# Local layers: token shift in front of the layer norm by two SBUF-to-SBUF copies in place of two matmuls, layer norm on whole rows

## The reference

```python
def shift_token(t):
    t1, t2 = jnp.split(t, 2, axis=-1)
    t2 = jnp.pad(t2, ((0, 0), (1, 0), (0, 0)))[:, :-1]
    return jnp.concatenate([t1, t2], axis=-1)

def _layer(x, wqkv, qs, ksc, wo, lg, lb, w1, b1, w2, b2):
    h = shift_token(x)
    qkv = h @ wqkv
    ...
    o = local_attention(q, k, v)
    x = x + o @ wo
    h = shift_token(x)
    mu = h.mean(-1, keepdims=True)
    var = h.var(-1, keepdims=True)
    h = (h - mu) / jnp.sqrt(var + 1e-05) * lg + lb
    h = h @ w1 + b1
    a, g = jnp.split(h, 2, axis=-1)
    h = a * jax.nn.gelu(g, approximate=False)
    x = x + h @ w2 + b2
    return x
```

## Time and profile before

| what | value |
|---|---|
| runs shown (us) | 3350.12, 3350.09, 3436.24 |
| median | 3350.12 us |
| profiled execution | 3355.18 us |
| its span, first to last instruction | 3353.0 us |
| TensorE busy | 3150.6 us (94%) |
| VectorE busy | 2405.7 us (72%) |
| ScalarE busy | 1821.5 us (54%) |
| GpSimd busy | 1577.1 us (47%) |
| granted TensorE clock, mean | 0.980 |
| DMA, local layers | load and store of 512 KB pieces, 16 passes |

### The profile page before, as it was taken

How to read it: one execution, slowest core, us unless ns; L and a number is a source line. 1 busy time by engine, 2 the same in 40 slices (tenths; PEclk the granted TensorE clock), 3 DMA queues, 4 the chain that set the end, 5 groups by cost and what they waited for, 6 DMA issues and landing times. The chain is left out here.

```text
span 3353.0 us, 51248 instructions
## 1 busy us (share of the span) xinstructions
PE 3150.6 (94%) x16012; PEld 1862.8 (56%) x16012; DVE 2405.7 (72%) x4374; ACT 1821.5 (54%) x4275; POOL 1577.1 (47%) x969
## 2 busy tenths in 40 slices
PE   6999999999999888999999799999999999999997
PEld 3454545454454545666666466666666666666665
DVE  8999999999999897667777555555555555555553
ACT  4768686777768545555656344444444444433442
POOL 2666666666666560000000355544555455555552
PEclk8999999999999999999999899999999999999999
DMA  4767677576767573000100000000001100000000
GB/s 148 259 215 246 220 239 240 210 267 213 258 217 241 204 234 124 25 25 25 38 31 13 20 1 19 19 19 19 19 19 38 57 19 25 25 25 25 25 13 19
DMA packets 146655, 343.30 MB, mean 102 GB/s; under 512 B 14898, under 2 KB 78470, under 8 KB 146582
## 3 DMA queue, kind: packets, MB, share of 16 engines
q1 hardware_dynamic: 138134, 334.02, 29.6%
q10 hardware_dynamic: 8448, 8.39, 0.8%
HBM read 320.87 MB, written 21.50 MB: 102 GB/s over the span
## 5 line engine op out<-in xcount | busy, mean ns | idle before, releaser
L559 POOL TENSOR_TENSOR hb<-bcB,du 128x1024 f32<-128x1024 f32 x256 | 602.1, 2352 | 390.1 <-DVE hb L699 350.9
L688 DVE TENSOR_TENSOR_SCAN ps_dA<-ps_dA,hb 128x1024 f32<-128x1024 f32 x256 | 585.8, 2288 | 43.6 <-ACT ps_dA L914 43.6
L1226 PE MATMUL ps_y<-hb,ident 128*128 128x512 f32 x1024 | 491.5, 609 | 28.9 <-DVE hb L699 28.9
L2077 POOL TENSOR_TENSOR c_pr<-c_pr,c_inv 128x512 f32<-128x512 f32 (+1 forms) x256 | 233.5, 933 | 364.6 <-DVE c_inv L2194 364.6
L1609 ACT ACTIVATE b_pr<-b_ps_s,b_negmax 128x256 f32<-128x256 f32 (+1 forms) x512 | 263.4, 527 | 166.7 <-DVE b_negmax L1522 165.3
L1226 PEld LDWEIGHTS ps_y<-hb,ident 128*128 128x128 f32 x1024 | 191.4, 194 | 252.8 <-issue 190.8
L914 ACT ACTIVATE ps_dA<-delta,a_neg 128x511 f32<-128x511 f32 x512 | 330.1, 676 | 1.1
L2313 ACT ACTIVATE c_pr<-c_ps_s,c_negmax 128x256 f32<-128x256 f32 (+1 forms) x512 | 224.8, 457 | 179.0 <-DVE c_negmax L2187 178.2
L699 DVE TENSOR_TENSOR hb<-ps_dA,bcC 128x1024 f32<-128x1024 f32 x256 | 311.9, 1218 | 5.9
L2187 DVE CUSTOM_DVE_ANT_0 c_ps_s<-c_ps_s,c_mask 128x256 f32<-128x256 f32 (+1 forms) x512 | 187.6, 417 | 120.4 <-issue 120.4
L2569 PE MATMUL c_ps_s<-c_hT,c_w 128*128 128x512 f32 x576 | 261.1, 600 | 0.9 <-ACT c_hT L2369 0.9
(11 more groups left out here) (295 smaller groups left out, 6177.1 us busy)
## 6 DMA issues: line engine op xcount, KB each, us to landing
bcB<-bc_scratch SPq DMA_DIRECT2D x256, 512.0 KB, 4.6
bcC<-bc_scratch SPq DMA_DIRECT2D x256, 512.0 KB, 4.7
c_x<-stream_scratch SPq DMA_DIRECT2D x16, 512.0 KB, 5.1
c_xr<-stream_scratch SPq DMA_DIRECT2D x16, 512.0 KB, 4.3
rows<-in_x_dram SPq DMA_DIRECT2D x8, 512.0 KB, 5.6
sum<-in_x_dram SPq DMA_DIRECT2D x8, 512.0 KB, 7.7
x_scratch<-sum SPq DMA_DIRECT2D x8, 512.0 KB, 6.7
b_xb<-x_scratch SPq DMA_DIRECT2D x8, 512.0 KB, 4.7
```

Of the source, the lines that this page charges most:

```text
L559: pool.tensor_tensor(hb[:, s % RING, :, :], bcB[:, s % ROWS, :, :], bc(du[:, c % 2, :].unsqueeze(1), [P, NG, T]), ALU.mult)\
L688: dve.tensor_tensor_scan(flat(h_all), flat(h_all), flat(tile), 0.0, ALU.mult, ALU.add)\
L1226: last = pe.matmul(ps_y[:, :], W["ident"][:, :], hb[:, r % RING, i, :], start=False, stop=(g == GROUPS - 1 and i == NG - 1))
L2077: pool.tensor_tensor(rows, rows, bc(inv[:, u, :].unsqueeze(2), [P, 2, w]), ALU.mult)\
```

## The change

The right half of the sum now goes to a tile of its own, `xa_right`, the left half straight into `h`. SyncE issues two copies from SBUF to SBUF: partitions 0 to 126 of `xa_right` to partitions 1 to 127 of `h`'s right half, and partition 127 of tiles 0 to 2 to partition 0 of tiles 1 to 3. The zeros of the first token are written once at the start. VectorE waits for both copies before any statistics, and takes statistics and normalisation on whole rows of 256, four instructions each. The two matmuls, their two matrices and the wait in front of them are gone. GpSimd's `residual` adds the two halves apart. In the diff, hunks that only rename the start-up semaphore's count on other engines are left out.

```diff
@@ -1895,12 +1895,11 @@
         den = sb("c_den", [P, UNITS, 2])
         inv = sb("c_inv", [P, UNITS, 2])
         tiny = sb("c_tiny", [P, 2, NH])
-        down = sb("c_down", [P, P])
-        corner = sb("c_corner", [P, P])
         oT = sb("c_oT", [P, IC, T])
-        xa = sb("c_xa", [P, TT, D])
+        xa_right = sb("c_xa_right", [P, TT, P])
+        h = sb("c_h", [P, TT, D])
         xa2 = sb("c_xa2", [P, TT, D])
-        stats = sb("c_stats", [P, TT, 12])
+        stats = sb("c_stats", [P, TT, 6])
         mv = sb("c_mv", [P, TT, 2])
         rstd = sb("c_rstd", [P, TT])
         veps = sb("c_veps", [P, TT])
@@ -1914,9 +1913,9 @@
         ps_o = ctx.enter_context(nc.psum_tensor("c_ps_o", [P, 2, 512], F32))
         ps_x = ps_t[:, :, :].rearrange("p a (b d) -> p (a b) d", b=2)
         ps_y = ps_o[:, :, :].rearrange("p a (b d) -> p (a b) d", b=2)
-        xsh = ps_t[:, 0, :].rearrange("p (t d) -> p t d", t=TT)
 
         s_c = ctx.enter_context(nc.semaphore("c_const"))
+        CONSTANTS = 6
         rot_ready = ctx.enter_context(nc.semaphore("c_rot_ready"))
         x_in = S("c_x_in", 16, "sp")
         xr_in = S("c_xr_in", 16, "sp")
@@ -1948,13 +1947,13 @@
         oT_ready = S("c_oT_ready", IC, "act")
         wo_done = S("c_wo_done", 1, "pe")
         xa_ready = S("c_xa", 2, "dve")
-        shifted = S("c_shifted", 1, "pe")
-        v_steps = S("c_v_steps", 2 * TT + 1, "dve")
+        shifted = S("c_shifted", 32, "sp")
+        v_steps = S("c_v_steps", TT + 1, "dve")
         mv_ready = S("c_mv", TT, "dve")
         g_steps = S("c_g_steps", 1, "pool")
         rstd_ready = S("c_rstd_ready", 1, "pool")
         xa2_ready = S("c_xa2", 1, "pool")
-        hn_ready = S("c_hn", 2 * TT, "dve")
+        hn_ready = S("c_hn", TT, "dve")
         h_turned = S("c_h_turned", DC, "pe")
         hT_ready = S("c_hT_ready", DC, "act")
         ag_proj = S("c_ag_proj", JC, "pe")
@@ -1962,7 +1961,7 @@
         hid_ready = S("c_hid", JC, "dve")
         y_done = S("c_y_done", 1, "pe")
         xo_ready = S("c_xo", 1, "dve")
-        b2_added = S("c_b2_added", 1, "pool")
+        b2_added = S("c_b2_added", 2, "pool")
         base_in = S("c_base_in", 16, "act")
         stored = S("c_stored", 16, "sp")
         block = ctx.enter_context(nc.Block())
@@ -2017,6 +2017,9 @@
                         sp.wait_ge(stored.s, stored.at(it - NB + 1, 16))
                     sp.dma_start(x_sb[:, :, :], tiles(stream[nl, nb])).then_inc(x_in.s, 16)
 
+                sp.wait_ge(xa_ready.s, xa_ready.at(it, 1))
+                sp.dma_start(h[1:P, :, P:D], xa_right[0:P - 1, :, :]).then_inc(shifted.s, 16)
+                sp.dma_start(h[0:1, 1:TT, P:D], xa_right[P - 1:P, 0:TT - 1, :]).then_inc(shifted.s, 16)
                 if l < L - 1:
                     sp.wait_ge(xo_ready.s, xo_ready.at(it, 1))
                     sp.dma_start(tiles(stream[l + 1, b]), xo[:, :, :]).then_inc(stored.s, 16)
@@ -2038,15 +2041,8 @@
             pool.memset(tiny[:, :, :], 1e-24).then_inc(s_c, 1)
 
             pool.memset(hid[:, JC - 1, :], 0.0).then_inc(s_c, 1)
-            pool.memset(down[:, :], 0.0).then_inc(s_c, 1)
-            pool.memset(corner[:, :], 0.0).then_inc(s_c, 1)
-            pool.wait_ge(s_c, 7)
-
-            pool.affine_select(out=down[:, :], in_=down[:, :], compare_op=ALU.not_equal, fill=1.0,
-                               base=1, pattern=[[-1, P]], channel_multiplier=1).then_inc(s_c, 1)
-            pool.affine_select(out=corner[:, :], in_=corner[:, :], compare_op=ALU.not_equal, fill=1.0,
-                               base=P - 1, pattern=[[1, P]], channel_multiplier=-1).then_inc(s_c, 1)
-            pool.wait_ge(s_c, 9)
+            pool.memset(h[0:1, 0, P:D], 0.0).then_inc(s_c, 1)
+            pool.wait_ge(s_c, CONSTANTS)
 
             def turn_heads(n, t):
 
@@ -2081,14 +2077,16 @@
                 pool.wait_ge(s_t, 16 * 15)
                 pool.wait_ge(xa_ready.s, xa_ready.at(it, 2))
                 pool.wait_ge(xo_ready.s, xo_ready.at(it, 0))
-                ins = pool.tensor_tensor(xa2[:, :, :], xa[:, :, :], bc(b2_row[:, l, :].unsqueeze(1), [P, TT, D]), ALU.add)
+                pool.tensor_tensor(xa2[:, :, P:D], xa_right[:, :, :], bc(b2_row[:, l, P:D].unsqueeze(1), [P, TT, P]), ALU.add)\
+                    .then_inc(b2_added.s, 1)
+                ins = pool.tensor_tensor(xa2[:, :, 0:P], h[:, :, 0:P], bc(b2_row[:, l, 0:P].unsqueeze(1), [P, TT, P]), ALU.add)
+                ins.then_inc(b2_added.s, 1)
+                pool.wait_ge(b2_added.s, b2_added.at(it, 2))
                 if l == L - 1:
-
-                    ins.then_inc(b2_added.s, 1)
-                    pool.wait_ge(b2_added.s, b2_added.at(it - (L - 1) * NB, 1))
                     pool.wait_ge(base_in.s, base_in.at(it - (L - 1) * NB, 16))
-                    ins = pool.tensor_tensor(xa2[:, :, :], xa2[:, :, :], xo[:, :, :], ALU.add)
-                ins.then_inc(xa2_ready.s, 1)
+                    pool.tensor_tensor(xa2[:, :, :], xa2[:, :, :], xo[:, :, :], ALU.add).then_inc(xa2_ready.s, 1)
+                else:
+                    pool.sem_inc(xa2_ready.s, 1)
 
             def root(it):
 
@@ -2231,25 +2229,22 @@
                 dve.wait_ge(xr_in.s, xr_in.at(it, 16))
                 dve.wait_ge(xa2_ready.s, xa2_ready.at(it, 0))
                 dve.wait_ge(hn_ready.s, hn_ready.at(it, 0))
-                for half in (slice(P, D), slice(0, P)):
-                    dve.tensor_tensor(xa[:, :, half], ps_x[:, :, half], xr[:, :, half], ALU.add).then_inc(xa_ready.s, 1)
+                dve.tensor_tensor(xa_right[:, :, :], ps_x[:, :, P:D], xr[:, :, P:D], ALU.add).then_inc(xa_ready.s, 1)
+                dve.tensor_tensor(h[:, :, 0:P], ps_x[:, :, 0:P], xr[:, :, 0:P], ALU.add).then_inc(xa_ready.s, 1)
 
                 st.turn(it)
                 dve.wait_ge(xa_ready.s, xa_ready.at(it, 2))
+                dve.wait_ge(shifted.s, shifted.at(it, 32))
                 for t in range(TT):
-                    st.done(dve.bn_stats(stats[:, t, 0:6], xa[:, t, 0:P]))
-                dve.wait_ge(shifted.s, shifted.at(it, 1))
-                for t in range(TT):
-                    st.done(dve.bn_stats(stats[:, t, 6:12], xsh[:, t, :]))
-                dve.wait_ge(st.s, st.at(2 * TT))
+                    st.done(dve.bn_stats(stats[:, t, :], h[:, t, :]))
+                dve.wait_ge(st.s, st.at(TT))
                 st.done(dve.memset(tick[:, :], 0.0))
                 for t in range(TT):
                     dve.bn_aggr(mv[:, t, :], stats[:, t, :]).then_inc(mv_ready.s, 1)
                 dve.wait_ge(rstd_ready.s, rstd_ready.at(it, 1))
                 for t in range(TT):
-                    for half, src in enumerate((xa[:, t, 0:P], xsh[:, t, :])):
-                        dve.tensor_scalar(hn[:, t, half * P:(half + 1) * P], src, mv[:, t, 0:1], rstd[:, t:t + 1],
-                                          ALU.subtract, ALU.mult).then_inc(hn_ready.s, 1)
+                    dve.tensor_scalar(hn[:, t, :], h[:, t, :], mv[:, t, 0:1], rstd[:, t:t + 1],
+                                      ALU.subtract, ALU.mult).then_inc(hn_ready.s, 1)
                 if more:
                     rotate(nl, n, 2)
                     rotate(nl, n, 3)
@@ -2540,15 +2535,11 @@
                     project_v(n, 0)
                     project_v(n, 1)
 
-                pe.wait_ge(xa_ready.s, xa_ready.at(it, 2))
-                pe.matmul(xsh, down[:, :], xa[:, :, P:D], start=True, stop=False)
-                pe.matmul(xsh[:, 1:TT, :], corner[:, :], xa[:, 0:TT - 1, P:D], start=False, stop=True)\
-                    .then_inc(shifted.s, 1)
                 if more:
                     project_qk(n, 2)
                     project_v(n, 2)
                     project_qk(n, 3)
-                pe.wait_ge(hn_ready.s, hn_ready.at(it, 2 * TT))
+                pe.wait_ge(hn_ready.s, hn_ready.at(it, TT))
                 for k in range(DC):
                     turn(ps_t[:, k, :], hn, k).then_inc(h_turned.s, 1)
                 if more:
```

More of the change, by code:

```diff
@@ L2005, in first @@
                 sp.wait_ge(W["b_stored"].s, W["b_stored"].at(NB, 0))
+                sp.wait_ge(s_c, CONSTANTS)
             def body(l, b, it, nl, nb):
@@ L2134, in _ @@
             dve.wait_ge(W["b_stored"].s, W["b_stored"].at(NB, 0))
-            dve.wait_ge(s_c, 9)
+            dve.wait_ge(s_c, CONSTANTS)
             dve.wait_ge(s_t, 16 * 15)
@@ L2280, in _ @@
             seed(act, sems["act"])
-            act.wait_ge(s_c, 9)
+            act.wait_ge(s_c, CONSTANTS)
             act.wait_ge(s_t, 16 * 15)
@@ L2397, in _ @@
             seed(pe, sems["pe"])
-            pe.wait_ge(s_c, 9)
+            pe.wait_ge(s_c, CONSTANTS)
             def turn(dst, src, k):
```

## The result

| kernel | median (us) | range of its runs (us) |
|---|---|---|
| before, beside it | 3350.11 | 3348.71 to 3350.12 (3 runs), and 3436.24 |
| changed | 3537.74 | 3536.09 to 3538.72 (4 runs) |

The ratio is 1.0561 (interval 1.0544 to 1.0578): the change makes the kernel slower by 187.6 us, where 189 were forecast. The fourth run of before, 2.6% above the other three, was in a slower state and isn't in the ratio. The profiled execution took 3537.47 us, with a span of 3535.7.

The account below looks back on a forecast made before the run. TensorE's stream was taken as the bound. Fifteen inner passes at 11.9 us (178), the last pass +12 and the start -1 sum to +189 us, taking the median of 3350.12 to 3539 us; range 3471 to 3679.

Parts of the forecast that it names:

- One engine for the first copy: The 127-row SBUF copy gets one DMA engine, since 127 is prime; one engine with streamed pieces has chance 0.84.
- Landing, 15.1 us: First copy, issue to arrival: 508 pieces at 26.5 ns make 13.5 us, plus 1.6 fixed; bounds 11.4 and 23.3.
- The chain behind the landing, 6.2 us: From landing to `hn` ready: statistics 1.40, aggregation and root 1.87, normalising 1.92 and 1.0; 6.2 us, before 6.72.
- `hn` late by 8.9 us: TensorE starts the `hn` transposes at 2527.6 in place of 2518.69, 8.9 us later, the saved 1.50 already inside.
- Clock, 3.0 us a pass: Behind each idle gap TensorE works some microseconds at a lower clock: 3.0 us a pass added, 2.4 to 3.6.
- An inner pass, 11.9: Each of 15 inner passes grows by 8.9 us of delay plus 3.0 of clock, 11.9 us; together 178 us.
- Last pass, +12.0: In the last pass `hn` is ready at 3325.9 against 3313.91, GpSimd's three adds each holding a normalising instruction: +12.0 us.
- Start, -0.9: At the start two fills and two selects leave GpSimd's list ahead of TensorE's first transpose: 0.9 us saved.
- Rival, spread and hidden, 3327: The copy spreads over 16 engines, lands in 3.0 us plus 0.4 and stays hidden: 3327 us, chance 0.09.
- The decision point of 4.7 us: Below 4.7 us of landing for the copy TensorE doesn't wait at all; the change breaks even at 6.2 us.
- Rival, a few engines, 3332: Say four engines carry the copy: landing 5.0 us, a wait of 0.3, about 3332 us; chance 0.03.
- The residual's split and the second copy at nothing: GpSimd's two half-size residual adds, and the 3-piece second copy one or two packets behind the first, cost nothing.

Follow-up runs that it names:

- e1: The changed kernel with its first copy cut into two on the same queue, 112 rows and 15 rows; 3328.05 us, ratio 0.9933.
- e6: The changed kernel with 11 more TensorE matmuls, results unread, before the wait for `hn` in each of 15 inner passes; 3505.03 us, ratio 1.0463.
- e7: The changed kernel without the two copies and their waits, right half written straight into `h`, so no token shift; 3324.88 us, ratio 0.9925.

## Why the prediction was right

The direction, the mechanism and the sum held: 3539 us were forecast and 3537.74 measured. Some terms did not hold, and two of them cancelled.

- **One engine for the first copy**: right. One mark and 20 GB/s for 508 pieces, and the cuts at 126, 124, 122 and 112 gave 14, 4, 2 and 16 engines. The rule of the Trainium skill (page "DMA: Bandwidth & Descriptors", section "Why a DMA increments its semaphore by 16 and not by 1"), quoted ahead of the result, now has the case that no trace of before could show, 127 rows: one engine.
- **Landing, 15.1 us**: 15.74 in the pass shown, 15.9 in the mean. The split of it was off in both parts: 395 packets in 10 us are 25.3 ns a piece, not 26.5, so 508 take 12.9 us; what is left, 2.9 us, is the fixed part that was put at 1.6 from a copy of 64 KB. The first data show some 1.5 us behind the issue, and for 2 us the rate is 8 to 15 GB/s before it reaches 20. The estimate of 11.6 us, which the prediction worked out from the fit in the Trainium skill (same page, section "Anatomy of one DMA"), was too short by 4 us; the page gives that fit for copies that GpSimd issues, and this one is SyncE's.
- **The chain behind the landing, 6.2 us**: from 2585.88 to 2592.05 it is 6.17. Statistics 1.41, 1.81 from their end at 2587.29 to the first normalising instruction at 2589.10, then 2.95 with one of the four held by `scale_heads`.
- **`hn` late by 8.9 us**: 9.46 in the pass shown (22.69 less 13.23), and the difference of 0.6 is that of its landing.
- **Clock, 3.0 us a pass**: too high. A pass takes 100.41 us against 87.23 in e1; less the mean wait of 11.0 that leaves 2.2, and e6 gives 2.2 by another way. The step that failed is the middle of three losses, 2.4, 3.6 and 3.0 us. The smallest came from the gap of 4.46 us that lies inside running work, as the new gaps do; the other two stand at the start of the layers and in the last pass. The row nearest in kind would have been the better term, though it is seen only afterwards. In an inner pass 1.6 us stand between the transposes and the hidden layer (4.35 in place of 2.75 us); the other 0.6 are not placed in single rows.
- **An inner pass, 11.9**: 11.7. The two errors, +0.6 and -0.8, nearly cancel, so the close sum is in part luck. It is no proof of the terms.
- **Last pass, +12.0**: 12.8. The three held instructions were right (5.35 us for the four; 4.7 and 0.4 forecast), the landing late by the same 0.6.
- **Start, -0.9**: 0.9 less was measured up to the first add, of which only 0.3 is the shorter GpSimd list (TensorE's first transpose idles 4.13 us in place of 4.46). Another 0.5 are these eight transposes, 1.48 us in place of 1.97; in e7, which has the same short list, they take 1.94, so that part is not the change's. The number came out by luck.
- **Rival, spread and hidden, 3327**: it is what e1 measures, 3328.05, so its price was right and only its condition was not met (it had the last pass unchanged within 0.3; from its add to the end it takes 1.3 us more). The decision point of 4.7 us is 4.9 in three kernels with waits.
- **Rival, a few engines, 3332**: badly priced. Four engines gave 3386, 54 us more. Its step "127 x 26.5 ns + 1.6 = 5.0" was short by 2.0 us in the first layer and by more in the second, and it charged no clock loss behind a wait of a few microseconds. This did no harm only because it was not the case.
- **The residual's split and the second copy at nothing**: right in the order as written; TensorE's waits for GpSimd's softmax product are unchanged at 19.4 us. What it did not foresee is that the second copy's issue is held for 11.3 us.

## What to carry over

Before replacing a matmul by a copy, look at the number of rows the copy has: a prime such as 127 (from a shift by one in 128 partitions) leaves it to one DMA engine, and 112 + 15 rows cost one issue more of 0.7 us and take 3.5 us in place of 15.7. Price such a copy by what the bounding engine has left to do until it needs the data, here 4.9 us of landing; within that it is free, and beyond it every microsecond counts once for the wait, and the idle stretch costs something more in the matmul clock (1.1 us behind 2.5, about 2 behind 4.3 and behind 11). On a queue, issue the copy that takes longest first (worth 0.7 us a pass here), and look at what stands behind it.

## What was not expected of the hardware

- The issue of a small copy behind a 508-piece copy on one engine held the SyncE queue for 11.3 us; behind 488 pieces on two engines for 4.6 us; behind 496 on four for 0.8 to 1.3; behind 448 on 16 for 0.9. Issued ahead of the large one it took 0.74, and the large copy behind it 0.73. The next issue behind the large copy was then the held one: a load of 512 KB, for 10.7 to 11.2 us. Nothing waited for it here.
- Four engines with 124 rows landed at 7.04 us, and at 7.7 to 8.1 where a load of 512 KB is issued 3 to 4 us behind, where their number alone gives less than 6. Their rate was 60 GB/s at first, then 26 to 46, and near 80 only for 0.6 us.
- The clock's price in the inner passes depends little on the length of the gap from 4.3 us on (2.0 us behind 4.3, 2.2 behind 11.0, in the mean of 15 passes), and keeping TensorE busy with idle matmuls gave back all of it. Behind a single gap in the last pass it varies by more than a microsecond (8.60 to 10.12 us for the same 16 matmuls), and not by the length of the gap: behind 25.2 us both 9.08 and 10.12 were measured.
